# An edge loop with its softmax keys read from a table, one softmax bank, three product banks, and scores summed two items at a time

## The reference

```python
q, k, v = x @ Wq + bq, x @ Wk + bk, x @ Wv + bv       # per node, in 8 heads of 32
e = edge_attr @ We                                    # per edge
kj = k[src] + e
alpha = einsum('ehc,ehc->eh', q[dst], kj) / sqrt(32)  # one score per edge and head
ea = exp(alpha - segment_max(alpha, dst)[dst])        # softmax over the edges of a target
alpha = ea / (segment_sum(ea, dst)[dst] + 1e-16)
msg = (v[src] + e) * alpha
out = segment_sum(msg, dst) + (x @ Ws + bs)
x = x + out                                           # then the experts, unchanged here
```

## Time and profile before

| what | us |
|---|---|
| median of the runs | 2565.55 |
| span of the profiled execution | 2568.6 |
| TensorE busy | 2382.9 |
| VectorE busy | 2037.0 |
| GpSimd busy | 1811.8 |
| ScalarE busy | 1577.5 |

### The profile page before, as it was taken

The page is one execution under the profiler, slowest core; times in us unless marked ns, Lnnn a source line. Parts: engine busy times, 40 slices in busy tenths (PEclk is TensorE's granted clock), DMA queues, the critical chain, the costliest instruction groups (busy, mean ns, idle before and its releaser), DMA issues. The chain is left out here.

```text
span 2568.6 us, 67072 instructions
## 1 busy us (share of the span) xinstructions
PE 2382.9 (93%) x13310; PEld 1992.2 (78%) x13311; DVE 2037.0 (79%) x5261; ACT 1577.5 (61%) x4373; POOL 1811.8 (71%) x2136
## 2 busy tenths in 40 slices
PE   6998999999999999999999999999995657999998
PEld 2445788888888888888888888888883646999998
DVE  6865899999999999999999999999997773222222
ACT  1222677777777677777767777767774224666665
POOL 4123788888888888888888888888886104666666
PEclk9999999999999999999999999999998557999999
DMA  7326777777777777777777777777772753433443
GB/s 229 128 107 187 231 227 221 227 228 228 223 227 227 220 230 224 221 227 226 227 221 226 227 225 229 227 218 220 228 223 78 227 162 60 71 63 64 70 66 55
DMA packets 337693, 476.68 MB, mean 186 GB/s; under 512 B 61318, under 2 KB 268492, under 8 KB 337052
## 3 DMA queue, kind: packets, MB, share of 16 engines
q0 software_dynamic: 92576, 259.72, 37.8%
q1 hardware_dynamic: 238492, 213.23, 28.0%
q10 hardware_dynamic: 6288, 0.05, 0.1%
HBM read 425.40 MB, written 50.57 MB: 185 GB/s over the span
## 5 line engine op out<-in xcount | busy, mean ns | idle before, releaser
L809 POOL DMA_INDIRECT kv_ring<-vk_table,tab_c x880 | 860.6, 978 | 284.3 <-issue 208.2
L963 PE MATMUL ps_e<-we_sb,aT 128*128 128x256 f32 x3520 | 919.5, 384 | 27.9 <-DVE ve_ke L1050 21.6
L963 PEld LDWEIGHTS ps_e<-we_sb,aT 128*128 128x128 f32 x3520 | 601.0, 191 | 102.8 <-issue 48.6
L1044 DVE TENSOR_TENSOR ve_ke<-kv_ring,ps_e 128x512 f32<-128x512 f32 x880 | 599.9, 682 | 38.1 <-PE ps_e L967 24.0
L1014 PE MATMUL ps_u<-ve_ke,sel 128*128 128x264 f32 x1760 | 547.7, 393 | 20.3 <-DVE node_slots L1114 6.8
L819 POOL TENSOR_TENSOR ve_ke<-ve_ke 128x256 f32<-128x256 f32 x880 | 553.4, 633 | 18.5 <-ACT factor L936 4.9
L967 PE MATMUL ps_e<-q_slots,selT 128*128 x1760 | 517.6, 375 | 0.0
L896 ACT COPY aT<-ps_t 128x256 f32<-128x256 f32 x880 | 325.5, 370 | 310.1 <-PE ps_t L951 189.6
L1114 DVE SCALAR_TENSOR_TENSOR node_slots<-node_slots,same_tile,ps_u 128x264 f32 x880 | 423.0, 481 | 29.5 <-DVE node_slots L1099 10.6
L967 PEld LDWEIGHTS ps_e<-q_slots,selT 128*128 128x128 f32 x1760 | 335.1, 190 | 45.9
L1032 DVE TENSOR_REDUCE alpha<-ve_ke 128x8 f32<-128x256 f32 x880 | 365.3, 415 | 5.6 <-issue 3.6
(11 more groups left out here) (249 smaller groups left out, 2642.3 us busy)
## 6 DMA issues: line engine op xcount, KB each, us to landing
a_ring<-in_edge_attr SPq DMA_DIRECT2D x880, 128.0 KB
loc_c<-loc_table SPq DMA_DIRECT2D x220, 128.0 KB
kv_ring<-vk_table,tab_c POOLq DMA_INDIRECT x880
vk_table<-kv_out SPq DMA_DIRECT2D x49, 256.0 KB
skip_table<-skip_out SPq DMA_DIRECT2D x49, 128.0 KB
skip<-skip_table SPq DMA_DIRECT2D x7, 896.0 KB, 10.8
xn_table<-node_slots SPq DMA_DIRECT2D x7, 896.0 KB, 6.5
out<-node_slots SPq DMA_DIRECT2D x1, 6144.0 KB
```

Of the source, the lines that this page charges most:

```text
L809: g.indirect_dma_start(out=kv_ring[:, i % N_KV, :], out_offset=None, in_=vk_table, in_offset=bass.IndirectOffsetOnAxis(ap=tab_c[:, c % N_T ...
L963: t.matmul(ps_e[i % 2][:, 0:D], aT[i % 2][:, k * P:(k + 1) * P], we_sb[:, k, :], start=(k == 0), stop=(k == KD - 1))
L1044: v.tensor_tensor(ve_ke[:, to:ke + 1:ke - to, 0:D], kv.rearrange("p (t d) -> p t d", t=2), e[:, None, :].to_broadcast([P, 2, D]), ALU.add) ...
```

## The change

First, the first and last run key of every item and head is computed once in the node stage, kept in two small tables in memory (`first_keys`, `last_keys`), and read for each chunk by two transfers that copy one row to all partitions (`load_keys`). The three turns on TensorE in slot 0 and ScalarE's copy of the last key are gone. Second, the softmax uses one PSUM bank in place of two, and the bank set free makes `ps_e` three banks. Third, VectorE sums the scores of two items in one instruction, with four buffers for the products. Fourth, VectorE's work per item is put in another order: in odd slots the adding to the running sum stands between the 512-column add and the multiply, and both reads of the next two target tiles stand in even slots.

```diff
@@ tables, written in the node stage
+        first_keys = dram("first_keys", (IT, H))
+        last_keys = dram("last_keys", (1 + IT, H))
...
+        key_c = [sb(f"key_c{i}", [P, KW], F32, c_soft) for i in range(2)]
...
+        def load_keys(sp, c):
+            first = first_keys[c * CH:(c + 1) * CH, :].rearrange("(o i) h -> o (i h)", o=1)
+            last = last_keys[c * CH:(c + 1) * CH + 1, :].rearrange("(o i) h -> o (i h)", o=1)
+            sp.dma_start(key_c[c % 2][:, 0:P], first.to_broadcast([P, P])).then_inc(keys_loaded[c % 2], 16)
+            sp.dma_start(key_c[c % 2][:, P:KW], last.to_broadcast([P, P + H])).then_inc(keys_loaded[c % 2], 16)
...
+                        sp.wait_ge(keys_ready, 3)
+                        to_table(first_keys, key_x[:, 0, :, :])
+                        to_table(last_keys[1:1 + IT, :], key_x[:, 1, :, :])
+                        sp.dma_start(last_keys[0:1, :], no_key[:, :]).then_inc(tables_written, 16)
...
-                        v.tensor_scalar(run_f, run_g[:, :, :], BIG, None, ALU.mult).then_inc(tables_ready, 1)
+                        then(v.tensor_scalar(run_f, run_g[:, :, :], BIG, None, ALU.mult))
+                        dve.sem_inc(tables_ready, 1)
+                        for k, col in enumerate((0, P - 1)):
+                            v.tensor_tensor(key_x[:, k, :, :], run_f[:, :, col:col + 1].to_broadcast([P, IB, H]),
+                                            head_row[:, None, :].to_broadcast([P, IB, H]), ALU.add).then_inc(keys_ready, 1)
@@ buffers of the edge loop
+            N_E = 3
+            N_KE = 4
...
-            ps_e = [ps3(f"ps_e{i}", [P, 512]) for i in range(2)]
+            ps_e = [ps3(f"ps_e{i}", [P, 512]) for i in range(N_E)]
-            ps_ak = ps3("ps_ak", [P, 512])
-            ps_rx = ps3("ps_rx", [P, 512])
...
+            ps_s = ps3("ps_s", [P, 512])
+            ps_a = ps_x = ps_s[:, 0:P]
+            ps_r, ps_d = ps_s[:, P:P + KW], ps_s[:, P + KW:P + KW + H]
@@ SyncE, slot 0 of a chunk
+                            load_keys(sp, c)
@@ ScalarE
-                            act.wait_ge(s["keyed"], at("keyed", c - 1))
+                            act.wait_ge(keys_loaded[1 - par], 32 * ((c - 1) // 2 + 1))
...
-                            nc.scalar.activation(not_f[:, :], ps_k, ACT.Abs, scale=-1.0, bias=run[:, 0:1])
...
-                            nc.scalar.copy(key_prev[:, :], run[:, P - 1:P]).then_inc(s["key_kept"], 1)
+                            keys = key_c[1 - par][:, :]
+                            nc.scalar.activation(not_f[:, :], keys, ACT.Abs, scale=-1.0, bias=run[:, 0:1])
@@ TensorE
-                    pe.wait_ge(s["ve_added"], at("ve_added", c * CH + (i - 2)))
-                    pe.wait_ge(s["kq_ready"], at("kq_ready", c * CH + (i - 2)))
+                    to = ps_e[(c * CH + i) % N_E]
+                    pe.wait_ge(s["ve_added"], at("ve_added", c * CH + (i - N_E)))
+                    pe.wait_ge(s["kq_ready"], at("kq_ready", c * CH + (i - N_E)))
...
-                            t.transpose(ps_k[:, KW - P:KW], key_prev[:, 0:1].to_broadcast([P, P]), ident[:, :])
-                            t.transpose(ps_k[:, 0:P], run[:, 0:1].to_broadcast([P, P]), ident[:, :])
-                            t.transpose(ps_k[:, P:2 * P], run[:, P - 1:P].to_broadcast([P, P]), ident[:, :]).then_inc(s["keyed"], 1)
...
-                            pe.wait_ge(s["keys_apart"], at("keys_apart", c - 1))
+                            pe.wait_ge(s["ea_ready"], at("ea_ready", c - 2))
                             t.transpose(ps_a, am[:, :], ident[:, :]).then_inc(s["scores_turned"], 1)
...
-                            pe.wait_ge(s["owned"], at("owned", c - 1))
+                            pe.wait_ge(s["shifted_ready"], at("shifted_ready", c - 1))
                             t.matmul(ps_d, min_f[:, 0:1].to_broadcast([P, P]), ident[:, 0:H], start=True, stop=False)
@@ VectorE
-                    v.tensor_reduce(alpha[par][:, i * H:(i + 1) * H], by_head(ve_ke[:, 2 * CH + i % 2, 0:D], C), AX_X,
+                def reduce_pair(c, par, i):
+                    dve.wait_ge(s["kq_ready"], at("kq_ready", c * CH + i + 1))
+                    ke = 2 * CH + i % N_KE
+                    v.tensor_reduce(alpha[par][:, i * H:(i + 2) * H], ve_ke[:, ke:ke + 2, 0:D].rearrange("p t (h c) -> p t h c", c=C), AX_X,
...
-                    meanwhile()
-                    if i:
-                        reduce(c, par, i - 1)
+                    between(i)
                     dve.wait_ge(s["ve_added"], at("ve_added", c * CH + i))
...
+                    def between(slot):
+                        if slot % 2 == 1:
+                            if slot in at_slot:
+                                add_next(*at_slot[slot])
+                        else:
+                            load_for(slot)
+                            if slot > 0:
+                                reduce_pair(c, par, slot - 2)
+                            load_for(slot + 1)
```

More of the change, by code:

```diff
@@ L135, in gnn_ffn @@
         run_loaded = [sem(f"run_loaded{i}", c_soft) for i in range(2)]
+        keys_loaded = [sem(f"keys_loaded{i}", c_soft) for i in range(2)]
         reset_loaded = [sem(f"reset_loaded{i}", c_soft) for i in range(2)]
@@ L229, in gnn_ffn @@
             resets_ready = sem("resets_ready", c1)
+            keys_ready = sem("keys_ready", c1)
             tail_zeroed = sem("tail_zeroed", c1)
@@ L251, in gnn_ffn @@
             assert TAB_OUT < NT - 6
+            TABLE_WRITES = 2 + 5 * (2 if n_last else 1)
             def rows_in(b, total=IT):
@@ L324, in _ @@
                 sp.wait_ge(stored[1], 16 + 32 * (NT // 2))
-                sp.wait_ge(tables_written, 16 * (1 + 3 * (2 if n_last else 1)))
+                sp.wait_ge(tables_written, 16 * TABLE_WRITES)
             @block.gpsimd
@@ L1015, in emit @@
                                      start=True, stop=True).then_inc(s["summed"], 1)
-                over_chunks(pe, emit, what="sum", parts={0: "keys", 3: "scores", 6: "minima", 10: "turn_scores"})
+                over_chunks(pe, emit, what="sum", parts={3: "scores", 6: "minima", 10: "turn_scores"})
             @block.vector
@@ L1026, in _, with score @@
                 v.memset(min_l[1][:, :], BIG).then_inc(s["setup"], 1)
[L1027 to L1032 removed]
+                dve.wait_ge(s["setup"], 4)
+                def reduce_pair(c, par, i):
+                    dve.wait_ge(s["kq_ready"], at("kq_ready", c * CH + i + 1))
+                    ke = 2 * CH + i % N_KE
+                    v.tensor_reduce(alpha[par][:, i * H:(i + 2) * H], ve_ke[:, ke:ke + 2, 0:D].rearrange("p t (h c) -> p t h c", c=C), AX_X,
                                     ALU.add).then_inc(s["alpha_ready"], 1)
[L1035 to L1036 removed]
+                def score(c, par, i, between):
+                    e, q = [ps_e[(c * CH + i) % N_E][:, k * D:(k + 1) * D] for k in range(2)]
                     kv = kv_ring[:, i % N_KV, :]
@@ L1117, in emit, with load_for @@
                 def emit(c, par, steps):
-                    adds = [(b, k) for kind, k, b in steps if kind == "add"]
-                    places = max(1, len([1 for kind, k, b in steps if kind == "score"]))
+                    scored = any(kind == "score" for kind, i, back in steps)
+                    adds = [(i, back) for kind, i, back in steps if kind == "add"]
+                    at_slot = {(i + LAG["add"]) % CH: (i, back) for i, back in adds}
                     tiles = []
-                    def load_next(place):
-                        if len(adds) > 0 and place + len(adds) >= places:
-                            b, k = adds.pop(0)
-                            tiles.append(node_tile_of(c - b, k))
+                    def load_for(slot):
+                        if slot in at_slot:
+                            i, back = at_slot[slot]
+                            tiles.append(node_tile_of(c - back, i))
@@ new lines, in add_next @@
+                    def add_next(i, back):
+                        n = tiles.pop(0)
+                        before = last_tile[0] if last_tile else n
+                        if i == 0:
+                            rescale(c - back, before)
+                        add(c - back, i, n, before)
+                        last_tile[:] = [n]
+                    def between(slot):
+                        if slot % 2 == 1:
+                            if slot in at_slot:
+                                add_next(*at_slot[slot])
[4 more added lines that the diff above has]
+                            load_for(slot + 1)
@@ L1128, in emit @@
                     for kind, i, back in steps:
                         if kind == "score":
-                            score(c, par, i, lambda: load_next(i))
+                            score(c, par, i, between)
                         elif kind != "add":
                             softmax(c, par, kind)
-                        else:
-                            if not tiles:
```

(12 more changed lines are left out.)

55 lines of the change are left out of this document (22 added, 33 removed).

## The result

The changed kernel takes 2604.03 us (median of 4 runs, 2601.77 to 2605.84), beside 2565.01 us for the kernel before: 1.0147 times as long (95% interval 1.0135 to 1.016, as in all brackets behind a ratio below). It is slower by 39 us, where 21 us less were forecast. The profiled execution has a span of 2604.1 us. The kernel before ran beside each group of the experiments too, so these are compared by their ratio to it.

A forecast was written before the change was run, and what follows sets the result against it. VectorE was taken as the bound outside stretch A, GpSimd and TensorE within it. 54 chunks x (0.09 + 0.26) = 19 us, plus 3, less 1, saves 21: 2544.5 us; own range 2532 to 2556, 8 in 10 2514 to 2562.

The forecast's parts named there:

- New order in odd slots: VectorE's running sum ahead of the multiply: a late TensorE sum could delay it in slot 3; cost nothing, little to spare.
- Wide sum: VectorE's 512-column score sum takes 0.60 us, saving 0.06 a pair; only 0.09 us a chunk counts, outside stretch A.
- the drain estimate: Each VectorE sum costs its whole duration: 0.148 us saved a pair, 65 us in all, about 2500 us; chance 0.01.
- Stretch A: Slot 1's add to slot 4's: stays 5.57 us, set by GpSimd and TensorE; VectorE waits 0.68 instead of 0.29.
- First rival: All VectorE's saving counts: stretch A shrinks to VectorE's 4.89 us, 37 us more saved, 2508 us; chance 0.12.
- Third bank: TensorE gains a slot of lead on products; VectorE's excess in slots 11 to 13 goes, 0.26 us a chunk.
- Second rival: VectorE's odd-slot running sums wait for late TensorE sums; stretch A grows 0.1 to 0.3 us, about 2564 us; chance 0.12.
- Sequencer: Both target-tile reads unhidden in VectorE's 8 even slots cost 0.80 us a chunk: 24 us slower, 2590 us; chance 0.05.
- Keys: TensorE's 0.34 us a chunk saved is hidden; SyncE's two extra transfers are covered by 6 us a chunk of waiting.
- Node stage: Small adds and a wait on VectorE, short issues on SyncE: costs 1 us, from 0 to 4.
- the 3 us for rarer stalls: Gain from TensorE's extra lead hiding rarer stalls: 3 us, out of VectorE's 12.3 us of waits for products.

The follow-up runs named there:

- experiments 1: Changed kernel with the softmax factor that the rescale multiplies by in the softmax PSUM bank instead of SBUF: 2575.15 us, ratio 1.0036.
- kernel 6: Changed kernel with the softmax factor and the forward scan's result in the softmax PSUM bank instead of SBUF: 2563.57 us, ratio 0.9992.
- experiment 5: Changed kernel with GpSimd's mask ahead of the gather of item 5 instead of behind it: 2567.59 us, ratio 1.0008.
- experiment 3: Changed kernel with all running sums and the rescale moved back behind the multiply, as in the kernel before: 2620.31 us, ratio 1.021.
- kernel 11: Kernel 7 with a ring of five gathered items in place of four: 2492.49 us, ratio 0.9701.
- experiment 8: Kernel before with only the softmax factor moved from SBUF to PSUM: 2553.6 us, ratio 0.996.
- the ring: Five buffers for gathered items in place of four, an edit made in kernel 11 (2492.49 us), 12 (2539.84 us) and 13 (2533.02 us).
- 12: Kernel 6 with a ring of five gathered items, GpSimd's mask one program step later so it starts when it did with four: 2539.84 us, ratio 0.9894.
- 13: Kernel before with factor in PSUM, GpSimd's mask ahead of the gather of item 5, and a ring of five gathered items: 2533.02 us, ratio 0.9867.
- experiment 2: Changed kernel with only the rescale and slot 13's running sum moved back behind the multiply: 2597.42 us, ratio 1.0122.
- kernel 7: Changed kernel with factor and forward scan in PSUM and GpSimd's mask ahead of the gather of item 5: 2542.12 us, ratio 0.9905.

## Why the prediction was wrong

The step that failed is "New order in odd slots ... Nothing, but with little to spare". I looked there for a late TensorE sum and priced the rescale and the backward scan as moving at their old length. In the new order they stand elsewhere against GpSimd's program, and the rescale's second instruction became 0.65 us longer and the scan 0.18; experiments 1 and 6 take that away and give 40 us. The first pages of this document have the engines meet only at semaphores; here two of them met without one. That L1098 lasted 0.565 us on average in the kernel before and 0.418 at its shortest was there to be read.

The rule stands in the Trainium skill, SBUF — State Buffer, section SBUF: two separate sides: a VectorE instruction with two SBUF inputs and a GpSimd instruction that reads SBUF share a port pair, and whoever comes second waits for the whole of the other. For the weighing the trace agrees: of 50 backward scans in the changed kernel 45 began inside a weighing, and 44 of these were held, to 0.29 us behind its end; the 45th began 0.06 before that end, and of the 5 others none was held. The other way round it shows too: in the kernel before, 44 weighings began 0.03 to 0.09 us after the backward scan and lasted 0.74 to 0.79 us, where their median is 0.62 and the longest in kernel 6 is 0.64. So the scan was free there because it came just ahead, as in this chunk of the kernel before. For the gathers the rule doesn't fit (see the last section).

```profile
1170.61 0.42 DVE L1064 TENSOR_TENSOR_SCAN scan_b<-resets,scan_f 128x128 f32<-128x128 f32 x1
```

```profile
1170.67 0.76 POOL L819 TENSOR_TENSOR ve_ke<-ve_ke 128x256 f32<-128x256 f32 x1
```

- Wide sum: right. 0.60 from start to start, 401 of 0.680 us in the stretch; the drain estimate is out. It took one sentence of the Trainium skill, VectorE: DVE Perf Modes, section The DRAIN you can't avoid, without the end of its paragraph, by which a next operation that is not held starts earlier; the trace agrees with that end (0.60 behind a sum of 0.68).
- Stretch A: right, 5.56, and experiment 5 shows that the mask's place sets it. But VectorE's idle time stands almost all before slot 3's running sum (0.43 by the median) and hardly before slot 4's add (0.06), where I had put it.
- First rival (A at 4.89): its price was right, 4.91 and 36 us, its condition wasn't met by the change itself.
- Third bank: right. Slots 11 and 12 alternate, the bank waits are gone.
- Second rival (late running sums in odd slots): its sign came, in slot 3, but it cost nothing: A stayed 5.56, and experiment 3 has the opposite sign.
- Sequencer: not in every even slot, but in slot 4 two reads come late instead of one (0.05 and 0.07 us by the starts), about 4 us more. In kernel 11, where slot 4's add no longer waits, both are hidden (0.59 and 0.59 from start to start).
- Keys: free by the waits (1.7 us for edge rows), as forecast, but nearer to the edge than "6 us a chunk" of SyncE's waiting says: a second pair of loads cost 38 us. No kernel here is the changed one without the loads.
- Node stage: within its 0 to 4 us. The first add of the edge loop starts at 226.8 to 229.5 us in the four kernels with the old node stage and at 229.4 to 231.9 in the eleven with the new one, 2.7 later by the means.

The holds are not the whole. The kernel before had some of them too (experiment 8: 10 us), and set beside kernel 8, kernel 6 is still 8 us slower (0.9992 against 0.996), where the forecast had the change 21 us faster. Kernel 6 is 19 us above the forecast by the medians, and 13 by the profiled spans (2560.7 against 2547.6). The term of the sum that this points at is the 3 us for rarer stalls, which were to shrink. By the slots, over 54 chunks, the medians of kernel 6 add up to 0.32 us a chunk less than before, against 0.35 forecast; but what single chunks take above their medians grew from 0.40 to 0.56, 9 us more in place of 3 less, so that some 12 of the 13 lie there. From 300 to 1900 us 67 adds of kernel 6 began less than 0.15 us after their gather had landed, against 14 before, with 16.5 us of idle time ahead of these adds against 3.8. That all of the missing time is late gathers is argued from these traces and not shown: the ring takes all late gathers away, those of the kernel before too, and 12 and 13 gained alike.

## What to carry to other kernels

When instructions are moved, list for each engine pair what the moved one will now run beside, not only what it waits for; for VectorE instructions with two SBUF tensors look at GpSimd's work there. A group whose mean stood well above its minimum, with no idle time ahead of it, was being held here. Moving it was a gamble (experiment 2); giving it a PSUM operand brought it to its shortest each time (experiments 1, 6 and 8).

## What the runs showed of the hardware

- A held 128x8 instruction ended 0.03 us behind GpSimd's weighing, a scan or a 128x256 multiply 0.29 us.
- A gather on GpSimd (0.97 us) holds VectorE only from about a third of it on. In the traces of the two kernels, of the instructions with two SBUF tensors that began inside one, all 180 that began at most 0.31 us into it ran free, and all 46 that began 0.33 to 0.76 into it were held.
- Where the hold ends differs, and why stays open: L1114 was let go 0.26 to 0.29 us behind the gather's end, and L1115, which began 0.61 into it, in 34 chunks only behind the weighing that followed, though it had begun ahead of that.
- A VectorE instruction that needs the result of a 512-column add right ahead of it starts 0.715 us after the add's start, and one that doesn't 0.597 (medians, kernel 3).
- A gather landed 4.2 to 4.6 us after its start (the median, by kernel), with four buffers or five. From 300 to 1900 us VectorE's add found it landed less than 0.15 us before in 14 of some 800 cases in the kernel before, 52 in the changed one, 105 in kernel 7 and 1 in kernel 11.
